# Causal attention on one core: maxima per 512-key chunk with a correction on GpSimd, and orders written by a planner

## The chip, the cores and the metric

The kernel runs on one NeuronCore of a Trainium2 chip. The metric is the device time of one execution in microseconds (us), the median of three runs. Engines are named as in the profile: PE (TensorE), PEld (its weight loads), DVE (VectorE), ACT (ScalarE), POOL (GpSimd), SP (SyncE, which issues DMAs).

## The reference

The model is four residual layers on x of 2048 tokens by 128: softmax attention, a mixture-of-experts layer, linear attention, the experts again. Only the first is touched by the change:

```python
K = jnp.einsum('bpd,ihd->biph', x, W_K)      # 16 heads of 64; Q, V alike
scores = jnp.einsum('biph,biqh->biqp', K, Q)
scores = jnp.where(mask[None, None, :, :], scores, NEG_INF)   # causal
attn = jax.nn.softmax(scores / np.sqrt(d_head).astype(np.float32), axis=-1)
z = jnp.einsum('biph,biqp->biqh', V, attn)
out = jnp.einsum('bqf,df->bqd', z_flat, W_O)
x = x + out                                   # its input was layernorm(x)
```

## The kernel before

`attention` works on 8 pairs of heads, one after the other. Within a pair, `STEPS` = 8 steps `j` each take two rows of 128 queries (2j and 2j+1) for both heads: four units `u`. A row's keys 0 to its own are cut into chunks of 512 (`BANK`), so a unit has n = 1, 1, 2, 2, 3, 3, 4, 4 chunks in steps 0 to 7; a pair has 80 chunks with 34,816 columns.

A chunk's path is: *score* on PE (L438 and L441, the high and the low part of q by k, and L440, which adds the causal mask to the last chunk) into one of `RING` = 5 PSUM banks; its maximum on DVE (L265 into `cmax`); once a unit's chunks are all there, L268 makes `nmax`, the row's negated maximum; the exponentials on ACT (L358, into `prob`, with the sum of each chunk in `esum`). `prob` has two sets of four tiles, by the step's parity.

When a step's exponentials are done, its key *groups* of 256 keys follow, j+1 of them: *turn* (L451, four transposes for each head into PSUM bank 5 or 6), the copies of these into `probT` (ACT at L365 for head 0, DVE at L274 for head 1; two buffers for each head), and *value* (L468, four products with v that write 64 rows each, in PSUM bank 7). After the last group ACT copies z (L369, *leave*), PE multiplies with `wo_bd` (L476, *out*: two products of 256 columns, one half for each head, into bank 7 as well), and DVE scales each head's half by the reciprocal sum `rinv` and adds it to x (L293, four instructions).

The order on each engine is one list for all pairs (`issue_order`), by a fixed rule: step j-1's turns and values are spread evenly between the scores of step j and what follows. The next pair's projections (*project* L485, *vproject* L494) come after all scores of a pair. POOL makes constants at the start and then does nothing in this layer.

## Time and profile before

| | us |
|---|---|
| runs | 1418.26 median of 3 (1417.16 to 1418.97) |
| the profiled execution's own time | 1418.09 |
| span, from its first instruction to its last | 1416.4 |
| attention stage, main part | 34 to 1080 |
| PE busy over the span | 1241.6 (88%) |
| DVE, ACT, POOL busy | 959.1, 793.5, 144.2 |

The profile is of one execution. Its span is the time between the first and the last instruction; its own time is 1.7 us longer. Busy time of PE is the union of matmuls whose ends are modelled, so it says when PE had work and not how close it was to its peak. Idle time before an instruction is put down to the engine that released it.

### The profile page before, as it was taken

The page shows a single profiled execution, that of the slowest core. Times are in us where ns is not written, and L with a number is a line of the kernel's source. Part 1 is how long each engine was busy: PE and PEld are TensorE (multiplying, and loading weights), DVE is VectorE, ACT ScalarE, POOL GpSimd, SP SyncE. Part 2 cuts the span into 40 slices and gives each one's busy share as a digit, 9 for nine tenths or more (in the row PEclk, how much of TensorE's full clock was granted, in tenths as well). Part 3 has the DMA queues.
Part 4 walks back from the last instruction along what each step waited for, and adds up shares of the span by engine and source line. Part 5 has one row for each costly group of instructions (what it writes and reads, how often), then busy time and mean ns, then how long its engine had stood idle before and what let it go on. Part 6 is the DMA issues. An engine that isn't in the chain of part 4 may idle for free. (4 is left out here: it accounts for less than half of the span.)

```text
span 1416.4 us, 22644 instructions
## 1 busy us (share of the span) xinstructions
PE 1241.6 (88%) x7936; PEld 856.4 (60%) x7936; DVE 959.1 (68%) x2284; ACT 793.5 (56%) x2146; POOL 144.2 (10%) x174
## 2 busy tenths in 40 slices
PE   5999999999999999999999999999996294886285
PEld 3666666666667666666666576666664292443285
DVE  5776777677767767776777677667764263998254
ACT  5766566666657666666666666666652162232043
POOL 1000000000000000000000000000000553553433
PEclk9999999999999999999999999999996596997588
DMA  3950200020001002000200020020000121000023
GB/s 102 140 133 1 60 1 1 1 60 1 1 22 39 1 1 60 1 1 1 60 1 1 16 46 1 0 60 1 1 1 1 49 64 47 0 0 0 27 59 95
DMA packets 52677, 41.07 MB, mean 29 GB/s; under 512 B 14177, under 2 KB 41442, under 8 KB 52578
## 3 DMA queue, kind: packets, MB, share of 16 engines
q1 hardware_dynamic: 50018, 34.50, 11.6%
q0 software_dynamic: 2560, 5.26, 1.1%
q8 instruction: 60, 0.98, 0.3%
q14 instruction: 39, 0.32, 0.1%
HBM read 13.49 MB, written 9.48 MB: 16 GB/s over the span
## 5 line engine op out<-in xcount | busy, mean ns | idle before, releaser
L265 DVE TENSOR_REDUCE at_cmax<-at_ps 128x1 f32<-128x512 f32 (+3 forms) x576 | 350.0, 619 | 169.0 <-PE at_ps L441 167.5
L358 ACT ACTIVATE at_prob<-at_ps,at_nmax 128x512 f32<-128x512 f32 (+3 forms) x640 | 391.8, 622 | 56.4 <-DVE at_nmax L268 53.6
L451 PE MATMUL at_ps<-ident,at_prob 128*128 128x128 f32 x2176 | 307.2, 275 | 19.0 <-DVE at_probT L274 9.6
L451 PEld LDWEIGHTS at_ps<-ident,at_prob 128*128 128x128 f32 x2176 | 249.1, 140 | 91.5 <-issue 25.5
L468 PE MATMUL at_ps<-at_probT,at_v 128*64 128x256 f32 (+1 forms) x2304 | 295.0, 379 | 3.9 <-DVE at_probT L274 3.3
L365 ACT ACTIVATE at_probT<-at_ps 128x512 f32<-128x512 f32 (+1 forms) x288 | 165.3, 574 | 228.0 <-PE at_ps L451 226.5
L438 PE MATMUL at_ps<-at_k_st,at_q_parts 128*128 128x512 f32 (+3 forms) x640 | 283.4, 443 | 8.2 <-ACT at_prob L358 7.2
L441 PE MATMUL at_ps<-at_k_st,at_q_parts 128*128 128x512 f32 (+3 forms) x640 | 251.1, 394 | 0.0
L274 DVE COPY at_probT<-at_ps 128x512 f32<-128x512 f32 (+1 forms) x288 | 189.2, 657 | 69.3 <-PE at_ps L451 66.9
L468 PEld LDWEIGHTS at_ps<-at_probT,at_v 128*64 128x64 f32 x2304 | 141.7, 136 | 129.7 <-issue 51.4
L438 PEld LDWEIGHTS at_ps<-at_k_st,at_q_parts 128*128 128x128 f32 x640 | 120.8, 189 | 87.3 <-ACT at_prob L358 50.6
L358 ACT ACTIVATION_READ_ACCUMULATOR at_prob<-at_ps,at_nmax 128x1 f32 x640 | 130.4, 204 | 0.0
L441 PEld LDWEIGHTS at_ps<-at_k_st,at_q_parts 128*128 128x128 f32 x640 | 124.5, 195 | 1.5
L646 POOL IOTA f_xn<- 128x16 uint32 x2 | 0.4, 186 | 1078.2 <-POOLq L504 1069.5
L293 DVE SCALAR_TENSOR_TENSOR x<-at_ps,at_rinv,x 128x128 f32<-128x128 f32 x256 | 77.8, 346 | 21.1 <-PE at_ps L476 18.4
L797 ACT ACTIVATE f_hT<-f_ps,f_wfix 128x128 f32<-128x128 f32 x192 | 54.7, 370 | 35.6 <-PE f_ps L842 35.6
L476 PE MATMUL at_ps<-at_wo_bd,at_zT 128*128 128x256 f32 x256 | 67.1, 384 | 2.0 <-ACT at_zT L369 2.0
L835 PE MATMUL f_ps<-ident,f_xs 128*128 128x128 f32 x48 | 14.3, 299 | 56.7 <-DMA f_xs<-slots_in 56.7
L440 PE MATMUL at_ps<-at_maskb,at_identb 128*128 128x128 bf16 x256 | 58.9, 230 | 0.0
L757 DVE COPY f_wfix<-wall 128x1156 f32 x48 | 37.1, 773 | 27.3 <-issue 26.4
L842 PE MATMUL f_ps<-f_xsT,f_wfix 128*128 128x128 f32 x384 | 55.2, 291 | 0.1
L476 PEld LDWEIGHTS at_ps<-at_wo_bd,at_zT 128*128 128x128 f32 x256 | 46.4, 189 | 13.5 <-ACT at_zT L369 7.9
(184 smaller groups left out, 1254.0 us busy)
## 6 DMA issues: line engine op xcount, KB each, us to landing
at_q_parts<-at_q_parts SPq DMA_DIRECT2D x64, 256.0 KB, 4.3
f_xs<-slots_in SPq DMA_DIRECT2D x48, 64.5 KB, 1.9
slots_in<-zeros SPq DMA_DIRECT2D x2, 1536.0 KB, 19.0
wall<-in_L_ffn_w_dram SPq DMA_DIRECT2D x1, 2048.0 KB, 18.9
wall<-in_L_ffn_w_dram SPq DMA_DIRECT2D x4, 512.0 KB, 6.6
f_got<-slots_out SPq DMA_DIRECT2D x8, 256.0 KB, 3.6
out_dram<-x SPq DMA_DIRECT2D x4, 256.0 KB, 2.4
slots_out<-f_ys,f_back POOLq DMA_INDIRECT x48, 2.2
```

The costliest lines, as they stand in the source:

```text
L265: dve.tensor_reduce(cmax[:, u % SLOTS, c:c + 1], bank, AX.X, ALU.max).then_inc(s_cmax, 1)
L274: dve.tensor_copy(probT[1][n % 2][:, 0:w], turn_ps[1][:, 0:w]).then_inc(s_probT[1], 1)
L293: last = dve.scalar_tensor_tensor(x[:, 2 * j + i, :], o_ps[i][:, h * D:(h + 1) * D], rinv[:, j % 2, 2 * i + h:2 * i + h + 1], x[:, 2 * j + ...
L358: act.activation(prob[j % 2][u % 4][:, c * BANK:c * BANK + w], ring[k % RING][:, 0:w], ACT.Exp, bias=nmax[:, u % SLOTS:u % SLOTS + 1], acc ...
L365: act.activation(probT[0][n % 2][:, 0:w], turn_ps[0][:, 0:w], ACT.Copy).then_inc(s_probT[0], 1)
L438: pe.matmul(bank[:, 0:w], q_hi[h][:, r * P:(r + 1) * P], keys, start=True, stop=False)
L440: pe.matmul(bank[:, w - P:w], identb[:, :], maskb[:, :], start=False, stop=False)
L441: last = pe.matmul(bank[:, 0:w], q_lo[h][:, r * P:(r + 1) * P], keys, start=False, stop=True)
L451: last = pe.transpose(turn_ps[h][:, b * P:(b + 1) * P], prob[j % 2][2 * i + h][:, t * P:(t + 1) * P], ident[:, :])
L468: last = pe.matmul(z_ps[rows, to:to + w], v[:, t, rows], probT[h][n % 2][:, 2 * P * b:2 * P * b + w], start=t == 0, stop=last_tile)
L476: last = pe.matmul(o_ps[i], zT[j % 2][:, i * P:(i + 1) * P], wo_bd[:, pair, :, :].rearrange("f h d -> f (h d)"), start=True, stop=True)
L842: last = pe.matmul(ps[2 + c % 2][:, f * P:(f + 1) * P], wfix[k][:, f * P:(f + 1) * P], xsT[k][:, :], start=True, stop=True)
```

## The change

**Maxima by chunk.** DVE's maximum of a chunk goes straight to `nmax` and ACT's exponential of that chunk uses it, without waiting for the other chunks of the row. What that leaves wrong is put right before the transposes: when a step's maxima are all there, DVE takes the row's (*peak*), POOL subtracts (*gap*), ACT makes the factors exp(gap) (*factor*), POOL multiplies the chunk sums with them (*weigh*), DVE adds and inverts (*total*), POOL makes one factor for each chunk, which contains the reciprocal sum as well (*scale*), and POOL multiplies every chunk of `prob` in place (*fix*, 80 for each pair, 640 in all). A turn waits for the fix of its columns.

**The output product.** Since `prob` is normalised, `wo_bd` becomes `wo`, the two products of *out* have 128 columns each, they go to a ring bank instead of bank 7, and DVE adds them with one instruction of 256 columns for each step.

**Orders and buffers.** `attention_plan` writes each engine's order from a table of steps, durations and priorities, over all pairs at once, so that steps of two pairs can mix. `probT` has `TURNED` = 4 buffers for each head. `run_of` returns one group, so each group's value products are a run of their own. The loops over the orders replace `run(order, pair, made)` on each engine.

```diff
--- before.py
+++ after.py
+RING = 5
+TURNED = 4
...
+    def run_of(j, g):
+        return [g]
...
+                w = width(u, c) / BANK
+                step(("score", p, u, c), "pe", 0.43 * w + 0.2 * (c == n - 1), ("sp", "second", p, row(u) // TPC))
+                step(("max", p, u, c), "dve", 0.15 + 0.54 * w, ("pe", "score", p, u, c), q > 1 and ("pool", "scale") + everything[q - 2])
+                step(("exp", p, u, c), "act", 0.42 + 0.42 * w, ("dve", "max", p, u, c),
+                     q > 1 and ("pe", "turn") + everything[q - 2] + (1, (j - 2) % STEPS))
+        last = ("act", "exp", p, 4 * j + 3, n - 1)
+        if n > 1:
+            step(("peak", p, j), "dve", 0.17, ("dve", "max", p, 4 * j + 3, n - 1))
+            step(("gap", p, j), "pool", 0.3, ("dve", "peak", p, j))
+            step(("factor", p, j), "act", 0.25, ("pool", "gap", p, j))
+            step(("weigh", p, j), "pool", 0.3, ("act", "factor", p, j), last)
+        step(("total", p, j), "dve", 0.35, ("pool", "weigh", p, j) if n > 1 else last)
+        step(("scale", p, j), "pool", 0.3, ("dve", "total", p, j))
+        for c in range(n):
+            for h in range(2):
+                for i in range(2):
+                    w = width(4 * j + 2 * i + h, c) / BANK
+                    step(("fix", p, j, c, h, i), "pool", 0.2 + 1.0 * w, ("pool", "scale", p, j), last)
+    groups = [(p, j, g) for p, j in everything for g in range(j + 1)]
...
+                n = groups.index((p, j, g)) - TURNED
+                step(("evict", p, j, h, g), reader, 0.16 + 0.42 * w if h == 0 else 0.14 + 0.55 * w, ("pe", "turn", p, j, h, g),
+                     n >= 0 and ("pe", "value") + groups[n][:2] + (run_of(*groups[n][1:])[-1],))
+            if g == run_of(j, g)[-1]:
+                step(("value", p, j, g), "pe", 0.85 * len(run_of(j, g)), ("act", "vproject", p, (2 * g + 1) // TPC),
+                     ("act", "evict", p, j, 0, g), ("dve", "evict", p, j, 1, g), q and ("act", "leave") + everything[q - 1])
...
+    urgent = {"pe": ["out", "project", "vproject", "score", "turn", "value"],
+              "act": ["factor", "leave", "evict", "vproject", "high", "exp"],
+              "dve": ["peak", "total", "evict", "low", "max", "add"],
+              "pool": ["gap", "weigh", "scale", "fix"], "sp": ["second"]}
...
+            s = min(ok, key=lambda s: (urgent[e].index(s[1]), can_start[s], s[2:]))
+            del can_start[s]
+            length = steps[s][0]
+            if e == "pe":
+                length += 0.16 * ((s[1] == "value") != (last == "value"))
+                last = s[1]
+                if s[1] in reader:
...
-        o_ps = [ps[RING + 2][:, 2 * D:4 * D], ps[RING + 2][:, 0:2 * D]]
...
-        wo_bd = sb("wo_bd", [P, PAIRS, 2, D])
+        wo = sb("wo", [P, PAIRS, D])
...
-        prob = [[sb(f"prob{k}{i}", [P, T - P * (i < 2)]) for i in range(4)] for k in range(2)]
+        prob = [[sb(f"prob{k}{i}", [P, T - P * (i < 2) - 2 * P * (k == 0)]) for i in range(4)] for k in range(2)]
...
-        probT = [[sb(f"probT{h}{k}", [P, BANK]) for k in range(2)] for h in range(2)]
+        probT = [[sb(f"probT{h}{k}", [P, BANK]) for k in range(TURNED)] for h in range(2)]
...
-                pool.memset(wo_bd[:, :, :, :], 0.0).then_inc(s_const, 1)
+
+                for it in order["pool"]:
+                    kind, p, j = it[:3]
+                    n, k, q = chunks(j), j % 2, STEPS * p + j
+                    if kind == "gap":
+                        pool.wait_ge(s_low, count_of["dve", "peak", p, j])
+                        pool.tensor_tensor(gap[:, k, :, 0:n], low[:, k, :].unsqueeze(2).to_broadcast([P, 4, n]), nmax[:, k, :, 0:n],
+                                           ALU.subtract).then_inc(s_gap, 1)
+                    elif kind == "weigh":
+                        pool.wait_ge(s_factor, count_of["act", "factor", p, j])
+                        pool.wait_ge(s_exp, count_of["act", "exp", p, 4 * j + 3, n - 1])
+                        pool.tensor_tensor(part[:, k, :, 0:n], factor[:, k, :, 0:n], esum[:, k, :, 0:n], ALU.mult).then_inc(s_part, 1)
+                    elif kind == "scale":
+                        pool.wait_ge(s_rinv, q + 1)
+                        share = rinv[:, k, :].unsqueeze(2).to_broadcast([P, 4, n])
+                        if n == 1:
+                            pool.tensor_copy(scale[:, k, :, 0:n], share).then_inc(s_scale, 1)
+                        else:
+                            pool.tensor_tensor(scale[:, k, :, 0:n], factor[:, k, :, 0:n], share, ALU.mult).then_inc(s_scale, 1)
+                    elif kind == "fix":
+                        _, _, _, c, h, i = it
+                        u = 2 * i + h
+                        w = width(4 * j + u, c)
+                        pool.wait_ge(s_scale, q + 1)
+                        cols = prob[k][u][:, c * BANK:c * BANK + w]
+                        pool.tensor_scalar(cols, cols, scale[:, k, u, c:c + 1], None, ALU.mult).then_inc(s_fix, 1)
...
-                            dve.tensor_reduce(cmax[:, u % SLOTS, c:c + 1], bank, AX.X, ALU.max).then_inc(s_cmax, 1)
-                            if c == chunks(u) - 1:
-                                dve.wait_ge(s_cmax, N_CMAX * pair + k + 1 - first_chunk[FIRST_MANY])
-                                dve.tensor_reduce(nmax[:, u % SLOTS:u % SLOTS + 1], cmax[:, u % SLOTS, 0:c + 1], AX.X, ALU.max,
-                                                  negate=True).then_inc(s_nmax, 1)
...
-                            for h, done in enumerate((s_acc1, s_acc2)):
-                                if h:
-                                    dve.wait_ge(s_acc1, STEPS * pair + j + 1)
-                                for i in range(2):
-                                    last = dve.scalar_tensor_tensor(x[:, 2 * j + i, :], o_ps[i][:, h * D:(h + 1) * D],
-                                                                    rinv[:, j % 2, 2 * i + h:2 * i + h + 1], x[:, 2 * j + i, :],
-                                                                    ALU.mult, ALU.add)
-                                last.then_inc(done, 1)
...
+                        dve.tensor_reduce(nmax[:, j % 2, u % 4, c:c + 1], bank, AX.X, ALU.max, negate=True).then_inc(s_max, 1)
+                    elif kind == "peak":
+                        j = it[2]
+                        n, k = chunks(j), j % 2
+                        dve.wait_ge(s_max, count_of["dve", "max", p, 4 * j + 3, n - 1])
+                        dve.tensor_reduce(low[:, k, :], nmax[:, k, :, 0:n], AX.X, ALU.min).then_inc(s_low, 1)
+                    elif kind == "total":
+                        j = it[2]
+                        n, k = chunks(j), j % 2
+                        if n == 1:
+                            dve.wait_ge(s_exp, count_of["act", "exp", p, 4 * j + 3, 0])
+                            dve.reciprocal(rinv[:, k, :].unsqueeze(2), esum[:, k, :, 0:1]).then_inc(s_rinv, 1)
+                            continue
+                        dve.wait_ge(s_part, count_of["pool", "weigh", p, j])
+                        dve.tensor_reduce(total[:, k, :], part[:, k, :, 0:n], AX.X, ALU.add).then_inc(s_total, 1)
+                        dve.wait_ge(s_total, count_of["pool", "weigh", p, j])
+                        dve.reciprocal(rinv[:, k, :], total[:, k, :]).then_inc(s_rinv, 1)
...
+                        dve.wait_ge(s_o, q + 1)
+                        if p:
+                            dve.wait_ge(s_add, q - STEPS + 1)
+                        rows = x[:, 2 * j:2 * j + 2, :]
+                        o = ring[use_of["out", p, j] % RING][:, 0:2 * D]
+                        dve.tensor_tensor(rows, o.rearrange("p (t d) -> p t d", d=D), rows, ALU.add).then_inc(s_add, 1)
...
+                        _, _, u, c = it
+                        j, h, w = u // 4, u % 2, width(u, c)
+                        if c == 0 and STEPS * p + j >= 2:
+                            act.wait_ge(s_turn[h], group(*divmod(STEPS * p + j - 1, STEPS), 0))
+                        act.wait_ge(s_max, count_of["dve", "max", p, u, c])
+                        act.activation(prob[j % 2][u % 4][:, c * BANK:c * BANK + w], ring[use_of["score", p, u, c] % RING][:, 0:w], ACT.Exp,
+                                       bias=nmax[:, j % 2, u % 4, c:c + 1],
+                                       accum_out=esum[:, j % 2, u % 4, c:c + 1]).then_inc(s_exp, 1)
+                    elif kind == "factor":
+                        j = it[2]
+                        n, k = chunks(j), j % 2
+                        act.wait_ge(s_gap, count_of["pool", "gap", p, j])
+                        act.activation(factor[:, k, :, 0:n], gap[:, k, :, 0:n], ACT.Exp).then_inc(s_factor, 1)
+                    elif kind == "evict":
+                        _, _, j, h, g = it
+                        n, w = group(p, j, g), turned(j, g) * P
+                        act.wait_ge(s_turn[0], n + 1)
+                        if n >= TURNED:
+                            act.wait_ge(s_value, value_run[n - TURNED])
+                        act.activation(probT[0][n % TURNED][:, 0:w], turn_ps[0][:, 0:w], ACT.Copy).then_inc(s_probT[0], 1)
...
+                        pe.wait_ge(s_fix, count_of["pool", "fix", p, j, 2 * g // TPC, h, 1])
+                        if n:
+                            pe.wait_ge(s_probT[h], n)
...
+                        pe.wait_ge(s_v, count_of["act", "vproject", p, (2 * end + 1) // TPC])
+                        if run_of(j, end)[0] == 0 and STEPS * p + j >= 1:
+                            pe.wait_ge(s_zT, STEPS * p + j)
+                        for h in range(2):
+                            pe.wait_ge(s_probT[h], group(p, j, end) + 1)
...
-                            for i in range(2):
-                                last = pe.matmul(o_ps[i], zT[j % 2][:, i * P:(i + 1) * P],
-                                                 wo_bd[:, pair, :, :].rearrange("f h d -> f (h d)"),
-                                                 start=True, stop=True)
-                            last.then_inc(s_o, 1)
...
+                            last = pe.matmul(ring[use_of[it] % RING][:, i * D:(i + 1) * D], zT[q % 2][:, i * P:(i + 1) * P], wo[:, p, :],
+                                             start=True, stop=True)
```

PE's order, first around the turns of step 3 of the first pair (L451 turn, L468 value, L438 and L441 score), before:

```order
L451 MATMUL at_ps<-ident,at_prob 128x128 x8
L438 MATMUL at_ps<-at_k_st,at_q_parts 128x512
L441 MATMUL at_ps<-at_k_st,at_q_parts 128x512
L451 MATMUL at_ps<-ident,at_prob 128x128 x4
L438 MATMUL at_ps<-at_k_st,at_q_parts 128x512
L441 MATMUL at_ps<-at_k_st,at_q_parts 128x512
L451 MATMUL at_ps<-ident,at_prob 128x128 x4
L468 MATMUL at_ps<-at_probT,at_v 64x256 x4
```

and now, the same step (L517 turn, L532 value, L505, L507 and L508 score, L542 out):

```order
L517 MATMUL at_ps<-ident,at_prob 128x128 x4
L542 MATMUL at_ps<-at_wo,at_zT 128x128 x2
L517 MATMUL at_ps<-ident,at_prob 128x128 x4
L505 MATMUL at_ps<-at_k_st,at_q_parts 128x512
L508 MATMUL at_ps<-at_k_st,at_q_parts 128x512
L517 MATMUL at_ps<-ident,at_prob 128x128 x4
L532 MATMUL at_ps<-at_probT,at_v 64x256 x4
L505 MATMUL at_ps<-at_k_st,at_q_parts 128x256
```

Where eight transposes stood in one run there are now two of four with *out* between them, and *out* has 128 columns instead of 256. Over the attention layer the runs of value products are 272 before and 285 now; those with a turn directly before them are 98 and 152, those with a turn directly behind them 42 and 89.

DVE's order, before (second pair, around the sums of step 4):

```order
L265 TENSOR_REDUCE at_cmax<-at_ps 128x1 x3
L268 TENSOR_REDUCE at_nmax<-at_cmax 128x1
L265 TENSOR_REDUCE at_cmax<-at_ps 128x1
L282 TENSOR_REDUCE at_rsum<-at_esum 128x4
L284 RECIPROCAL at_rinv<-at_rsum 128x4
L293 SCALAR_TENSOR_TENSOR x<-at_ps,at_rinv,x 128x128 x4
L265 TENSOR_REDUCE at_cmax<-at_ps 128x1 x2
L268 TENSOR_REDUCE at_nmax<-at_cmax 128x1
L274 COPY at_probT<-at_ps 128x512
```

and now, around the same sums:

```order
L371 COPY at_probT<-at_ps 128x512
L348 TENSOR_REDUCE at_nmax<-at_ps 128x1
L353 TENSOR_REDUCE at_low<-at_nmax 128x4
L371 COPY at_probT<-at_ps 128x384
L348 TENSOR_REDUCE at_nmax<-at_ps 128x1 x2
L362 TENSOR_REDUCE at_total<-at_part 128x4
L364 RECIPROCAL at_rinv<-at_total 128x4
L348 TENSOR_REDUCE at_nmax<-at_ps 128x1 x3
L380 TENSOR_TENSOR x<-at_ps,x 128x256
```

The reductions L268, one for each unit, are gone; in their place stand one `low` and one `total` for each step, and four scale-and-add instructions have become one.

POOL's order now, steps 6 and 7 of the second pair (before it has nothing here):

```order
L301 TENSOR_TENSOR at_gap<-at_low,at_nmax 128x16
L306 TENSOR_TENSOR at_part<-at_factor,at_esum 128x16
L313 TENSOR_TENSOR at_scale<-at_factor,at_rinv 128x16
L320 TENSOR_SCALAR at_prob<-at_prob,at_scale 128x512 x11
L301 TENSOR_TENSOR at_gap<-at_low,at_nmax 128x16
L320 TENSOR_SCALAR at_prob<-at_prob,at_scale 128x512
L320 TENSOR_SCALAR at_prob<-at_prob,at_scale 128x128
L320 TENSOR_SCALAR at_prob<-at_prob,at_scale 128x256
L320 TENSOR_SCALAR at_prob<-at_prob,at_scale 128x128
L320 TENSOR_SCALAR at_prob<-at_prob,at_scale 128x256
L306 TENSOR_TENSOR at_part<-at_factor,at_esum 128x16
L313 TENSOR_TENSOR at_scale<-at_factor,at_rinv 128x16
L320 TENSOR_SCALAR at_prob<-at_prob,at_scale 128x512 x9
```

The small steps of the next step stand between the fixes: *weigh* of the step with n = 4 waits for that step's last exponential, and the fixes behind it in the queue wait with it.

## Rows read from the trace of the kernel before

**Rows 1.** Stages: from:to, length, busy of PE, PEld, DVE, ACT, POOL, clock, DMA share.
```profile
34.00:1080.00 1046.00, 1006.98 (x6628) 680.75 (x6628) 744.43 (x1646) 672.22 (x1782) 0.19 (x1) 1.00 0.13 25
...
1160.00:1340.00 180.00, 117.11 (x464) 68.27 (x462) 125.41 (x303) 46.73 (x154) 77.77 (x94) 0.79 0.05 15
```
**Rows 2.** The same view, one head pair of 128 us.
```profile
280.00:408.00 128.00, 124.56 (x823) 84.44 (x822) 91.44 (x200) 83.69 (x222) 0.00 (x0) 1.00 0.08 17
```
**Rows 3.** Waits, 152 to 1040 us: total us, times, longest.
```profile
ACT at_prob L358 <- DVE at_nmax L268: 47.1, 58, 1.5
...
PE at_ps L451 <- DVE at_probT L274: 7.9, 10, 1.5
```
**Rows 4.** PE timeline, first and last of 2,020 rows: start us, length, instruction.
```profile
152.13 1.02 PE L485 MATMUL at_ps<-at_xnT,at_wT_q 128*128 128x512 f32 x2
...
1047.41 0.48 PE L441 MATMUL at_ps<-at_k_st,at_q_parts 128*128 128x512 f32 x1
```
**Rows 5.** The same view, 611 to 622 us.
```profile
612.34 0.39 PE L441 MATMUL at_ps<-at_k_st,at_q_parts 128*128 128x512 f32 x1
612.57 0.49 PE L451 MATMUL at_ps<-ident,at_prob 128*128 128x128 f32 x3
612.81 0.31 PE L438 MATMUL at_ps<-at_k_st,at_q_parts 128*128 128x128 f32 x1
...
613.15 0.51 PE L451 MATMUL at_ps<-ident,at_prob 128*128 128x128 f32 x3
613.59 1.08 PE L468 MATMUL at_ps<-at_probT,at_v 128*64 128x256 f32 x8
614.61 0.50 PE L438 MATMUL at_ps<-at_k_st,at_q_parts 128*128 128x512 f32 x1
614.94 0.40 PE L441 MATMUL at_ps<-at_k_st,at_q_parts 128*128 128x512 f32 x1
615.27 0.87 PE L468 MATMUL at_ps<-at_probT,at_v 128*64 128x256 f32 x8
616.07 0.50 PE L438 MATMUL at_ps<-at_k_st,at_q_parts 128*128 128x512 f32 x1
...
618.24 1.08 PE L476 MATMUL at_ps<-at_wo_bd,at_zT 128*128 128x256 f32 x4
619.15 0.60 PE L451 MATMUL at_ps<-ident,at_prob 128*128 128x128 f32 x4
```
**Rows 6.** Timeline of all engines, end of the attention stage.
```profile
1052.23 0.70 ACT L358 ACTIVATE at_prob<-at_ps,at_nmax 128x512 f32<-128x512 f32 x1
...
1063.97 1.08 PE L468 MATMUL at_ps<-at_probT,at_v 128*64 128x256 f32 x8
...
1064.99 1.09 PE L451 MATMUL at_ps<-ident,at_prob 128*128 128x128 f32 x8
...
1066.02 1.08 PE L468 MATMUL at_ps<-at_probT,at_v 128*64 128x256 f32 x8
...
1073.34 1.25 DVE L293 SCALAR_TENSOR_TENSOR x<-at_ps,at_rinv,x 128x128 f32<-128x128 f32 x4 [2.80 <-PE at_ps L476]
```
**Rows 7.** The same view, the opening.
```profile
21.55 5.27 PE L485 MATMUL at_ps<-at_xnT,at_wT_k 128*128 128x512 f32 x8 [2.44 <-ACT at_xnT L346]
...
36.75 0.30 PE L438 MATMUL at_ps<-at_k_st,at_q_parts 128*128 128x128 f32 x1 [0.37 <-issue]
```
**Rows 8.** Groups by line and shape, 34 to 1080 us: busy us, mean ns, idle before.
```profile
L293 DVE SCALAR_TENSOR_TENSOR x<-at_ps,at_rinv,x 128x128 f32<-128x128 f32 x256 | 77.8, 346 | 21.1 <-PE at_ps L476 18.4
...
L268 DVE TENSOR_REDUCE at_nmax<-at_cmax 128x1 f32<-128x4 f32 x64 | 10.1, 157 | 2.2
```
**Rows 9.** The same columns, GpSimd's groups of the whole span.
```profile
L968 POOL TENSOR_TENSOR li_outer<-li_qk,li_v 128x1152 f32<-128x1152 f32 x16 | 35.5, 2222 | 44.1 <-DVE li_qk L994 44.1
...
L962 POOL TENSOR_TENSOR li_state<-li_state,li_fresh 128x144 f32<-128x144 f32 x16 | 7.9, 491 | 1.7 <-POOL li_fresh L958 1.0
...
L43 POOL TENSOR_SCALAR_AFFINE_SELECT ident<-ident 128x128 f32<-128x128 f32 x1 | 0.3, 294 | 0.1
```

More of the change, by code:

```diff
@@ L71, in attention @@
-    N_V = NC
-    V_FIRST = N_SC + N_PJ
-    V_BANKS = [RING - 2, RING - 1] * (N_V // 2)
-    BANKS = [use % RING for use in range(V_FIRST)] + V_BANKS
-    def back_of(j):
-        items = []
-        for g in range(j + 1):
-            items += [("turn", j, 0, g), ("turn", j, 1, g)]
-            if g:
-                items += [("value", j, g - 1), None]
-        return items + [("value", j, j), None, ("leave", j)]
-    def spread(items, weights):
-        ends = [round(len(items) * sum(weights[:i]) / sum(weights)) for i in range(len(weights) + 1)]
-        return [items[a:b] for a, b in zip(ends, ends[1:])]
@@ L140, in attention @@
-    order, last_order = ([it for it in issue_order(projections) if it] for projections in (True, False))
-    opening = [(step, i) for i in range(N_PJ) for step in ("project", "low")] + [("vproject", m) for m in range(N_V)]
+    order, row, chunks, width, turned, run_of = attention_plan(PAIRS, NT, NC, TPC)
+    uses = [it for it in order["pe"] if it[0] in ("score", "project", "vproject", "out")]
+    use_of = {it: n for n, it in enumerate(uses)}
+    count_of = {}
+    for e in order:
+        ran = {}
+        for it in order[e]:
+            ran[it[0]] = ran.get(it[0], 0) + 1
+            count_of[(e,) + it] = ran[it[0]]
@@ L143, in attention, with group @@
+    def group(p, j, g):
+        return p * STEPS * (STEPS + 1) // 2 + j * (j + 1) // 2 + g
+    value_run = {}
+    for it in order["pe"]:
+        if it[0] == "value":
+            for g in run_of(it[2], it[3]):
+                value_run[group(it[1], it[2], g)] = count_of[("pe",) + it]
     with ExitStack() as ctx:
@@ L321, in _ @@
-                run(opening, 0, 0)
-                for pair in range(PAIRS - 1):
-                    run(order, pair, pair + 1)
-                run(last_order, PAIRS - 1, PAIRS)
+                    elif kind == "low":
+                        _, _, c, i = it
+                        cols = slice(c * BANK, (c + 1) * BANK)
+                        bank = ring[use_of["project", p, c, i] % RING]
+                        dve.wait_ge(s_hi, count_of["act", "high", p, c, i])
+                        for h in range(2):
+                            here, there = slice(DH * h, DH * (h + 1)), slice(DH * (1 - h), DH * (2 - h))
+                            if i == 0:
+                                last = dve.tensor_tensor(k_st[h][there, cols], bank[here, :], k_st[h][here, cols].bitcast(F32), ALU.subtract)
+                                continue
+                            last = dve.scalar_tensor_tensor(q_lo[h][here, cols], bank[here, :], SCALE, q_hi[h][here, cols].bitcast(F32),
+                                                            ALU.mult, ALU.subtract)
+                        last.then_inc(s_lo, 1)
@@ L497, in _ @@
[L497 to L500 removed]
+                        last.then_inc(s_value, 1)
+                    elif kind == "out":
+                        j = it[2]
+                        q = STEPS * p + j
+                        free_bank(it)
+                        pe.wait_ge(s_zT, q + 1)
+                        for i in range(2):
+                            last = pe.matmul(ring[use_of[it] % RING][:, i * D:(i + 1) * D], zT[q % 2][:, i * P:(i + 1) * P], wo[:, p, :],
+                                             start=True, stop=True)
+                        last.then_inc(s_o, 1)
+                    elif kind == "project":
+                        _, _, c, i = it
+                        free_bank(it)
+                        pe.matmul(ring[use_of[it] % RING][:, :], wT["kq"[i]][:, p, :], xnT[:, c * BANK:(c + 1) * BANK],
+                                  start=True, stop=True).then_inc(s_proj, 1)
+                    elif kind == "vproject":
+                        m = it[2]
+                        free_bank(it)
+                        for b in range(TPC):
+                            t = m * TPC + b
+                            last = pe.matmul(ring[use_of[it] % RING][:, b * P:(b + 1) * P], xnT[:, t * P:(t + 1) * P], wT["v"][:, p, :],
+                                             start=True, stop=True)
+                        last.then_inc(s_vproj, 1)
```

449 lines of the change are left out of this document (188 added, 261 removed).

## The prediction

> **What bounds the kernel now.** I read the busy time by stage first, then one head pair of it, the waits, and last the timeline of PE. The attention stage's main part takes 1046 us, 74% of the span, with PE busy for 1006.98, DVE for 744.43 and ACT for 672.22; the granted clock is 1.00, the upper of its two levels, so 2.4 GHz [rows 1]. Pairs repeat each 128 us: PE 124.56, DVE 91.44, ACT 83.69 of them [rows 2]. So this stage is bound by PE's queue, and DVE and ACT (71% and 65%) cost only where PE waits for them. A busy PE can also be one that starts its next matmul late. To see how much that is, I took all 2,020 merged rows of PE's timeline between 152 and 1048 us [rows 4], took the time from each start to the next, and sorted it by the pattern (what stood before, what runs, what follows). Taking a pattern's time at its fastest fifth as its price without waiting, the prices add up to 837 us and the excess over them to 58 us: 6.4%, 8.2 us of each pair, 66 us of the stage. The waits name the causes: ACT's exponentials for a row's maximum (47.1 us in all), which holds PSUM banks that PE wants, and PE's transposes for the copies out of the turn banks [rows 3]. The remaining 120 us of a pair are matmuls in order.
>
> **The change, part by part.**
>
> *The output product.* The two products of 256 columns take 0.91 us from start to start [rows 5]. Value products, also f32, do four of 256 columns in 0.80 us when two run side by side in the two halves of the array [rows 5], so one alone streams for about 0.40 to 0.43. Two of 128 columns then cost half of 0.86: 64 steps x 0.43 = **27 us off** PE, which is on the path for the whole stage. The bounds are 20 (the last step and the pair ends partly hide it) and 30.
>
> *Waits.* The exponential of a chunk no longer waits for its row; the copies have four buffers instead of two; *out* leaves bank 7, so that the next step's values need not wait for DVE's additions; DVE loses 192 small reductions of 157 ns (30 us) and changes 256 instructions of 346 ns (77.8 us busy) [rows 8] into 64 of twice the columns, at most 0.69 us each or 44 us. DVE goes from 92 us of a pair to about 84. Against that stand new waits of turns for POOL. The gain has the bounds 66 us (all waits gone) and minus 30 (below nothing: each of 64 steps may wait 0.5 us for the chain); I take **30 off**, a little under half of what is there, since the fix of a step can only start when its last exponential is done, which is a new late spot at each step.
>
> *Neighbours on PE.* Three transposes before a score cost 0.24 us (612.57 to 612.81) and before a value run 0.44; a value run then takes 1.02 with transposes before it and 0.80 in one place with a score before it, where the score pays 0.33 instead of 0.23 [rows 5]. Over the timeline a value run between scores took 0.80 in a third of the cases and 1.01 in the others, so moving a turn between score and values costs 0.22 in one third and nearly nothing in the rest: 0.1 us. The orders have 240 such neighbourhoods of turns and values instead of 140, and 13 more value runs at 0.35: 10 + 4.5, of which I take **10 on**; bounds 2 and 22. Turns among scores cost the same in any mix: by the patterns' prices eight transposes in a run and two scores behind them take 1.79 us, two runs of four with a score behind each 1.80 [rows 4].
> The Trainium skill, TensorEngine Tiling (Array Packing), Key Properties, says that changing the tiling mode drains TensorE, while another tile of the same mode does not. By that rule only value runs count (64 rows each), not who their neighbour is, and the term would be 13 x 0.35, about 4.5 us instead of 10; the rows agree on the drain at a value run but show the neighbour's price besides.
>
> *GpSimd's work.* No row shows a multiplication by a column of factors on POOL. The nearest are its tensor-tensor operations: 491 ns for 144 columns and 2222 for 1152 [rows 9], so 1.72 ns a column and 0.24 us fixed; 512 columns make 1.12 us. From below there is the select over 128 columns with one input in 0.29 us [rows 9], against 0.46 by the line: two thirds of it, 0.72 us. I take 1.1, the line, since it is a multiplication. A pair is 80 x 0.24 + 34,816 x 0.00172 = 79 us, plus 20 small steps at up to 0.46 = 9: 88 us of a pair, against some 118 of PE (120 without waits, 3.4 less for *out*, 1.3 more for neighbours). It is covered by PE's work, and while it is covered costs **nothing**. Without cover: step 7 alone is 16 x 0.24 + 7936 x 0.00172 = 17.5 us of fixes, and PE's turns and values of that step are 8 x 2.05 = 16.4 (1063.97 to 1066.02 is one group [rows 6]); the cover is the next pair's projections and scores.
> The Trainium skill, GPSIMD Engine Reference, Performance versus the Vector engine, has 769 ns measured for 512 elements of a tight loop with one input. An estimate by that figure makes POOL's pair 68 x 0.35, some 24 us, shorter, and the end below 16 x 0.35 or 5.6 us: the sum would come to 1364. No row here shows it.
>
> *The opening.* The first score starts at 36.75 us, 15.2 us after the first projection [rows 7], since all projections precede it. Now it waits only for the first chunk's. The same matmuls remain, so the gain is idle time alone: **4 off**, bounds 0 and 9.
>
> *The end.* In the last pair nothing follows step 7. From the last exponential's end (1052.9) to x (1074.6) it is 21.7 us [rows 6]. Now: *weigh* and *scale* at 0.49 each [rows 9] and two small steps of DVE at 0.16 [rows 8], 1.3; fixes 17.5; then the last turn 0.4, values 0.8 and *out* 0.5 [rows 5], two copies by ACT 1.0 and the addition 0.7 [rows 6, 8], 3.4: 22.2, and step 6's fixes may still be queued before: **3 on**, bounds 0 and 12.
>
> *At nothing:* *peak*, *gap*, *factor* (48 of each, beside exponentials; without that cover 0.16 + 0.49 us, and for the factor at most the 0.70 of an exponential of 512 columns [rows 6], 1.35 us a step, 65 us in all), the memset gone from POOL's start, and everything after the attention stage, where neither work nor order changes.
>
> Sum: -27 - 30 + 10 - 4 + 3 = -48 against the profiled execution's 1418.09, thus **1370 us**. The median of the runs is 1418.26, 0.2 us away, so nothing is corrected.
>
> **The rivals.**
>
> *POOL's chain eats the gain* (every step's first turn waits). In the order *weigh* of the next step stands before fixes of this one, and waits for the next step's last exponential. What speaks for it: the engines run their lists strictly in order, and the planner's durations (ACT 0.84 us for an exponential of 512 columns, a mask 0.2 us) aren't those of the trace. Against it: PE has scores to do meanwhile. Then the waits stay as they are or grow by some: 1400, between 1390 and 1416.
>
> *The plan works fully.* All old waits go, and new ones don't come, as the planner only places a turn where its fix is done: 30 us more off than forecast, 1340.
>
> *GpSimd becomes the bound: slower.* Mechanism: the fix takes longer than by the line, because POOL reads and writes SBUF while DVE is busy for 71% of the time (the rows of the line come from a stretch with DVE at 70% as well, 125.41 of 180 us [rows 1], which speaks against it), or because one input column by a factor is slower than two tensors. The place is steps 4 to 7, the large ones. With 9 us of small steps and 19.5 of fixed cost, PE's 118 us leave 2.57 ns a column: 1.56 us for 512 columns makes POOL the bound, and about 1.7 makes the kernel as slow as now. At 1.8 a pair is 134.6 us: 8 x 6.6 = 53 us on, and 16 x 0.7 = 11 more at the end: 1482. The Trainium skill, GPSIMD Engine Reference, Specifications, says that POOL's SBUF interfaces are shared with VectorE and names as contention DVE's instructions in a 2-port mode or with two SBUF inputs. By that rule DVE's work here, which reads PSUM with at most one SBUF input, would leave the fixes alone, and this rival would rest on the second cause only.
>
> *The change doesn't do what it says:* the value runs could be merged anyway or the orders alike; the orders above show that neither is so. No chance.
>
> **How the numbers follow.** Forecast 0.58, 1370; its own range, with the waits between 12 and 48 off and the other terms half way to their bounds, is 1345 to 1395. POOL's chain 0.17, the full plan 0.13, GpSimd as bound 0.12. The range that holds 8 in 10 takes in the chain and the plan and leaves GpSimd's bound out: 1335 to 1414. About 0.2% (2.8 us) is what a measurement of this kernel can tell from no change. Faster: all of the forecast and the plan, and most of the chain, 0.85; same 0.03; slower 0.12.
>
> **What would show it.** Right: the attention stage ends near 1030 instead of 1077, a pair takes about 122 us with PE's share at 97% or more, POOL busy for 75 to 90 us of it, the fix of 512 columns at 0.7 to 1.2 us, *out* at about 0.5 us, and PE's waits for `at_prob` from POOL few and short. Wrong: fixes at 1.5 us or more, turns that wait for POOL as the longest line of the waits, DVE's 512-column reductions longer than 686 ns, or ACT's exponentials later than before despite the chunk's own maximum.

## The result, and the profile after

The changed kernel takes 1441.43 us (median of 4 runs, 1440.2 to 1442.7) beside 1417.71 for the kernel before (median of 4): a ratio of 1.0167, 95% interval 1.0154 to 1.0179. It is 24 us slower; 1370 was forecast, the range ended at 1414, and the rival that came true had a chance of 0.12. The profiled execution has a span of 1441.0 us.

The page's busy times and two of its 40-slice lines:

```profile
PE 1229.0 (85%) x7936; PEld 837.6 (58%) x7936; DVE 891.8 (62%) x1948; ACT 797.3 (55%) x2192; POOL 1038.3 (72%) x973
...
PE   5899998999999999999999999999987194886375
...
POOL 0787879878996888798789968887993443554343
```

In the slices that lie wholly in the attention stage POOL is busy at 0.6 or more. A stretch of 130 us in it, by stage view (length, busy of PE, PEld, DVE, ACT, POOL, clock):

```profile
290.00:420.00 130.00, 121.66 (x807) 80.31 (x805) 81.04 (x154) 84.03 (x225) 110.87 (x100) 1.00 0.06 13
```

DVE went from 91.44 us in 128 [rows 2] to 81.04 in 130 and PE from 124.56 to 121.66: both have less to do in a pair, and the time is longer. POOL is busy for 110.87 of 130 us, 85%. Its groups by shape, in the columns of [rows 8]:

```profile
L320 POOL TENSOR_SCALAR at_prob<-at_prob,at_scale 128x512 f32<-128x512 f32 x448 | 694.3, 1569 | 4.7
L320 POOL TENSOR_SCALAR at_prob<-at_prob,at_scale 128x384 f32<-128x384 f32 x64 | 80.0, 1249 | 0.8
L320 POOL TENSOR_SCALAR at_prob<-at_prob,at_scale 128x256 f32<-128x256 f32 x64 | 59.7, 932 | 0.0
...
L320 POOL TENSOR_SCALAR at_prob<-at_prob,at_scale 128x128 f32<-128x128 f32 x64 | 39.1, 612 | 0.1
```

A fix of 512 columns takes 1569 ns where the forecast had 1.1 us. From 128 to 512 columns it is 957 ns more, 2.49 ns a column, with 0.29 us fixed. The tensor-tensor line of [rows 9] had 1.72 and 0.24. The waits of the whole span (total, times, longest), where [rows 3] stood before:

```profile
PEld at_ps L517 <- POOL at_prob L320: 122.8, 179, 1.9
...
POOL at_gap L301 <- DVE at_low L353: 55.7, 20, 5.1
...
PE at_ps L517 <- POOL at_prob L320: 50.3, 88, 1.5
...
ACT at_prob L423 <- DVE at_nmax L348: 41.7, 78, 1.4
...
POOL at_part L306 <- ACT at_prob L423: 26.9, 19, 2.6
```

The line that was named as a sign of failure is there: transposes (L517) that wait for POOL's `at_prob`, 50.3 us by PE's matmuls and 122.8 by its weight loads. The exponentials' wait for maxima is only a little lower: 41.7 us over the whole span, after 53.6 in the kernel before. POOL itself waits as well, for `low` at each step and for the last exponential. The end of the stage, in the columns of [rows 6]:

```profile
1066.81 0.67 ACT L423 ACTIVATE at_prob<-at_ps,at_nmax 128x512 f32<-128x512 f32 x1
...
1069.76 0.23 POOL L313 TENSOR_TENSOR at_scale<-at_factor,at_rinv 128x16 f32<-128x16 f32 x1
1070.09 24.06 POOL L320 TENSOR_SCALAR at_prob<-at_prob,at_scale 128x512 f32<-128x512 f32 x16
...
1082.51 1.09 PE L517 MATMUL at_ps<-ident,at_prob 128*128 128x128 f32 x8 [1.30 <-POOL at_prob L320]
...
1088.67 0.86 PEld L517 LDWEIGHTS at_ps<-ident,at_prob 128*128 128x128 f32 x8 [1.85 <-POOL at_prob L320]
1088.67 1.09 PE L517 MATMUL at_ps<-ident,at_prob 128*128 128x128 f32 x8 [1.39 <-POOL at_prob L320]
...
1099.22 0.42 DVE L380 TENSOR_TENSOR x<-at_ps,x 128x256 f32<-128x256 f32 x1 [2.37 <-PE at_ps L542]
```

After the last exponential (it ends at 1067.48) POOL does 16 fixes in 24.06 us, and PE starts transposes when it lets them: 1.30 and 1.39 us of idle time before them. From the last exponential's end to x it is 32.2 us, after 21.7 before. The first score, where [rows 7] has it at 36.75:

```profile
31.34 0.43 PE L505 MATMUL at_ps<-at_k_st,at_q_parts 128*128 128x128 f32 x1
```

Laid end to end: the first score comes 5.4 us earlier, the stretch from there to the last exponential's end is 20.0 longer (1036.1 after 1016.2), the end 10.5 longer: together 25 us, which is the whole difference of the spans (24.6). Behind the attention stage both traces have 341.4 us, so nothing there takes part.

One reading of the forecast must be mended first. A pair doesn't take 128 us. From the first projection of one pair to that of the next PE's timeline has 130.2 us in the kernel before, each time alike but for the first pair, and in the changed one 130.0 to 134.4 over the last five, a mean of 132.1. (A pair's length is taken over these last five in the experiments too.) By the same patterns and prices as in the forecast, PE's work of a pair is 121.8 us before and 118.7 now, and what goes beyond it 8.4 and 13.4. So the work fell by more than forecast (3.1 us for each pair; the forecast had 2.1) and the waits rose by 5 where they should have fallen by 3.7. How a pair splits into work and waits depends on how the patterns are drawn, by 1 to 2 us; that the waits rose does not. Of the 93 us beyond the prices in 919 us of this trace, 47 lie between a score and a turn.

### The profile page after: what moved, and what is told of

Read it like the earlier page. It is cut to its first block and busy times, and to the rows that moved or that the text cites. A ratio compares the mean times of both kernels' runs of the same rounds, so it can differ in the third digit from the quotient of the medians.

```text
span 1441.0 us, 24550 instructions
## 1 busy us (share of the span) xinstructions
PE 1229.0 (85%) x7936; PEld 837.6 (58%) x7936; DVE 891.8 (62%) x1948; ACT 797.3 (55%) x2192; POOL 1038.3 (72%) x973
## 5 line engine op out<-in xcount | busy, mean ns | idle before, releaser
L320 POOL TENSOR_SCALAR at_prob<-at_prob,at_scale 128x512 f32<-128x512 f32 (+3 forms) x640 | 867.0, 1377 | 5.6
L348 DVE TENSOR_REDUCE at_nmax<-at_ps 128x1 f32<-128x512 f32 (+3 forms) x640 | 376.8, 606 | 174.3 <-PE at_ps L508 171.1
L423 ACT ACTIVATE at_prob<-at_ps,at_nmax 128x512 f32<-128x512 f32 (+3 forms) x640 | 393.3, 624 | 42.8 <-DVE at_nmax L348 41.7
L517 PE MATMUL at_ps<-ident,at_prob 128*128 128x128 f32 x2176 | 338.5, 278 | 63.3 <-POOL at_prob L320 50.3
L517 PEld LDWEIGHTS at_ps<-ident,at_prob 128*128 128x128 f32 x2176 | 249.1, 140 | 188.5 <-POOL at_prob L320 122.8
L532 PE MATMUL at_ps<-at_probT,at_v 128*64 128x256 f32 (+1 forms) x2304 | 297.9, 380 | 3.9 <-DVE at_probT L371 3.0
L505 PE MATMUL at_ps<-at_k_st,at_q_parts 128*128 128x512 f32 (+3 forms) x640 | 283.9, 444 | 5.2 <-ACT at_prob L423 2.5
L508 PE MATMUL at_ps<-at_k_st,at_q_parts 128*128 128x512 f32 (+3 forms) x640 | 252.9, 395 | 0.0
L532 PEld LDWEIGHTS at_ps<-at_probT,at_v 128*64 128x64 f32 x2304 | 140.8, 136 | 111.1 <-issue 65.9
L505 PEld LDWEIGHTS at_ps<-at_k_st,at_q_parts 128*128 128x128 f32 x640 | 121.4, 190 | 69.8 <-issue 38.0
L508 PEld LDWEIGHTS at_ps<-at_k_st,at_q_parts 128*128 128x128 f32 x640 | 125.1, 195 | 1.6
L714 POOL DMA_INDIRECT slots_out<-f_ys,f_back x48 | 47.1, 981 | 63.6 <-DVE f_ys L823 51.0
L853 ACT ACTIVATE f_hT<-f_ps,f_wfix 128x128 f32<-128x128 f32 x192 | 54.7, 370 | 33.9 <-PE f_ps L898 33.9
L707 POOL DMA_INDIRECT slots_in<-f_xn,f_pos_u x32 | 31.4, 981 | 55.3 <-DVE f_pos_u L798 46.2
L1024 POOL TENSOR_TENSOR li_outer<-li_qk,li_v 128x1152 f32<-128x1152 f32 x16 | 35.5, 2220 | 43.1 <-DVE li_qk L1050 43.1
L507 PE MATMUL at_ps<-at_maskb,at_identb 128*128 128x128 bf16 x256 | 59.2, 231 | 0.0
```

The source lines that it names most:

```text
L320: pool.tensor_scalar(cols, cols, scale[:, k, u, c:c + 1], None, ALU.mult).then_inc(s_fix, 1)
L348: dve.tensor_reduce(nmax[:, j % 2, u % 4, c:c + 1], bank, AX.X, ALU.max, negate=True).then_inc(s_max, 1)
L423: act.activation(prob[j % 2][u % 4][:, c * BANK:c * BANK + w], ring[use_of["score", p, u, c] % RING][:, 0:w], ACT.Exp, bias=nmax[:, j % 2, ...
L505: pe.matmul(bank[:, 0:w], q_hi[h][:, r * P:(r + 1) * P], keys, start=True, stop=False)
L507: pe.matmul(bank[:, w - P:w], identb[:, :], maskb[:, :], start=False, stop=False)
L508: pe.matmul(bank[:, 0:w], q_lo[h][:, r * P:(r + 1) * P], keys, start=False, stop=True).then_inc(s_score, 1)
```

## The experiments

Each is an edit of the changed kernel, with the orders written anew by its planner where the plan is touched. The kernel before took 1417.15 to 1417.78 us beside them.

**1. Almost no work in the fixes (e1_narrow).**

```diff
-                        cols = prob[k][u][:, c * BANK:c * BANK + w]
+                        cols = prob[k][u][:, c * BANK:c * BANK + 1]
```

> Edit: each fix on GpSimd multiplies one column of its chunk instead of all (so most of the correction and of the normalisation is left out); orders, waits and small steps stay. Theory P (the time of the fixes, 1.57 us for 512 columns, holds up the transposes): PE's priced work of 118 us a pair remains and waits fall from 13 us a pair to 3 to 5, so 1350 to 1370 us. Theory C (the chain of small steps between the engines, not the fixes, makes the transposes late): the chain stays, 1415 to 1441. Theory O (the orders and their neighbours on PE cost more than before): 1425 or more.

Measured: 1374.08 us, ratio to the kernel before 0.9694 (0.9678 to 0.971). The fixes:

```profile
L320 POOL TENSOR_SCALAR at_prob<-at_prob,at_scale 128x1 f32<-128x1 f32 x640 | 164.5, 282 | 5.6
```

All waits, orders and small steps are the same; only the length of the fixes is gone, and with it 67 us. A pair takes 124.2 us. So neither the chain of small steps nor the orders make the kernel slower than before. The time stays 4 us above the expectation's upper end of 1370; no run here shows what these 4 us are. The edit also changes the values that the later layers get, but behind the attention stage this trace has 340 us, after 341 in the changed kernel.

**2. The fix in another form (e2_tt).** The output is complete here.

```diff
-                        pool.tensor_scalar(cols, cols, scale[:, k, u, c:c + 1], None, ALU.mult).then_inc(s_fix, 1)
+                        pool.tensor_tensor(cols, cols, scale[:, k, u, c:c + 1].to_broadcast([P, w]), ALU.mult).then_inc(s_fix, 1)
```

> Edit: the fix as a tensor-tensor multiplication with the factor broadcast along the row, same order. By the line through the tensor-tensor rows of the linear attention a fix of 512 columns takes 1.12 us instead of 1.57. Theory P: the waits fall to about 6 us a pair, 1375 to 1400 us. Theory C and O: 1430 to 1441. If the fix itself is no shorter in this form (1.5 us or more), the time says nothing on them and the line was a wrong guide.

Measured: 1373.83 us, ratio 0.9688 (0.9672 to 0.9704). The fixes and a stretch of 130 us:

```profile
L320 POOL TENSOR_TENSOR at_prob<-at_prob,at_scale 128x512 f32<-128x512 f32 x448 | 452.3, 1040 | 3.8
...
L320 POOL TENSOR_TENSOR at_prob<-at_prob,at_scale 128x128 f32<-128x128 f32 x64 | 25.6, 399 | 0.1
```

```profile
290.00:420.00 130.00, 127.11 (x869) 87.68 (x869) 85.19 (x163) 88.17 (x240) 77.29 (x104) 1.00 0.07 17
```

And the turns' waits for GpSimd over the whole span, 122.8 and 50.3 us in the changed kernel:

```profile
PEld at_ps L517 <- POOL at_prob L320: 21.3, 48, 1.3
...
PE at_ps L517 <- POOL at_prob L320: 2.4, 4, 0.8
```

The same multiplication with the factor as a broadcast second tensor takes 1040 ns for 512 columns, 1.67 ns a column: two thirds of the other form. The time is that of the first experiment within 0.3 us. PE's matmuls hardly wait for GpSimd any more. With fixes of 1.04 us GpSimd's work is thus covered, as the forecast had it for 1.1, and POOL is busy for 77 of 130 us. One line changed turns a loss of 24 us into a gain of 44.

**3. Only the plan knows the length (e3_replan).**

```diff
-                    step(("fix", p, j, c, h, i), "pool", 0.2 + 1.0 * w, ("pool", "scale", p, j), last)
+                    step(("fix", p, j, c, h, i), "pool", 0.3 + 1.27 * w, ("pool", "scale", p, j), last)
```

> Edit: the planner is given 0.3 + 1.27 us for a fix instead of 0.2 + 1.0, all orders are written anew; no instruction changes. If the wrong duration in the plan is what costs (PE stands before transposes that aren't ready while others could run), 1385 to 1410 us. If GpSimd's own load is the limit (88% of a pair and in series with each step's last exponential), 1425 to 1445.

Measured: 1423.49 us, ratio 1.0044 (1.003 to 1.0058): 18 us less than the changed kernel, and still slower than before. It fell 2 us below the range expected of a pure load and 13 above that of a pure planning error, so both take part: of the 67 us that slow fixes cost, 18 come from orders written for 1.2 us, and 49 stay when the orders know. A pair then takes 130.3 us.

**4. Two groups' value products in a run (e4_pairs).**

```diff
     def run_of(j, g):
-        return [g]
+        return list(range(g // 2 * 2, min(g // 2 * 2 + 2, j + 1)))
```

> Edit: two neighbouring key groups' value products in one run, orders planned for it. Per value run the drain costs about 0.3 us, and there are some 130 runs fewer: 40 us less work on PE. Theory P: PE waits for GpSimd instead, 1425 to 1441 us, waits a pair up by 3 to 5 us. Theory that PE is still the bound and its switches are what made the change slower: 1395 to 1405.

Measured: 1416.25 us, ratio 0.9989 (0.9979 to 0.9999). That is 25 us less than the changed kernel, between the two expectations, so it decides for neither alone. The runs of value products fall from 285 to 159. A pair is 129.2 us, 2.9 less, and the transposes still wait for GpSimd, from 150 to 970 us:

```profile
PEld at_ps L517 <- POOL at_prob L320: 70.6, 107, 1.4
...
PE at_ps L517 <- POOL at_prob L320: 38.8, 78, 1.1
```

**5. The same with the fast fix (e5_tt_pairs).** Both edits, of experiments 2 and 4.

> Edit: the fix as tensor-tensor multiplication (1.04 us for 512 columns in the run before) and value products of two key groups in one run, orders planned for it. With the slow fix the pairs gave 25 us (1441.4 to 1416.3). Theory P': with the fast fix PE is the bound, each drain spared counts in full, some 130 runs x 0.3 us = 40 us: 1330 to 1342 us. Rival: POOL's chain shows again as soon as PE is faster, 1350 to 1365.

Measured: 1339.98 us, ratio 0.9447 (0.9431 to 0.9463). From experiment 2 this is 33.9 us for 126 runs fewer, 0.27 us each, where slow fixes let only 25 through. Runs, their neighbours and the orders change together here, so the 0.27 us is not split among them. A pair takes 120.0 us, so POOL's chain does not show again.

**6. And the plan knows the fast fix (e6_tt_pairs_plan).**

```diff
-                    step(("fix", p, j, c, h, i), "pool", 0.2 + 1.0 * w, ("pool", "scale", p, j), last)
+                    step(("fix", p, j, c, h, i), "pool", 0.2 + 0.85 * w, ("pool", "scale", p, j), last)
```

> Edit: as the pairs with the fast fix, and the planner is given 0.2 + 0.85 us for a fix of 512 columns, what it takes, instead of 1.2. If only the load on GpSimd counts, the same as with the old duration within 3 us. If the plan's wrong durations cost something in either direction, 5 us or more faster.

Measured: 1329.94 us, the median of three executions of 1327.9 to 1330.3, ratio 0.9381 (0.9362 to 0.9399). A fourth took 5813, which nothing here explains and which the ratio leaves out; the median of all four is 1330.12. A wrong duration in the plan costs in this direction too: 10 us, 118.4 us a pair. It is the fastest version, 88 us below the kernel before and 111 below the changed one. Its page:

```profile
PE 1166.1 (88%) x7936; PEld 854.5 (64%) x7936; DVE 877.8 (66%) x1948; ACT 794.7 (60%) x2192; POOL 734.4 (55%) x973
...
PE   5999999999999999999999999999972867886195
...
POOL 0665566757555674675566476747634334552433
```

**7. A constant for the factor (e7_constant).** This leaves out the correction and the normalisation.

```diff
-                        pool.tensor_scalar(cols, cols, scale[:, k, u, c:c + 1], None, ALU.mult).then_inc(s_fix, 1)
+                        pool.tensor_scalar(cols, cols, 0.5, None, ALU.mult).then_inc(s_fix, 1)
```

> Edit: the fix multiplies by the constant 0.5 instead of a factor for each row from SBUF (the correction and the normalisation are left out), same order. If the operand from SBUF is what makes this form slow, 512 columns take 0.6 to 1.1 us and the kernel 1374 us; if it is the form itself, 1.5 to 1.6 us and 1441 us.

Measured: one execution, 1406.99 us. The fixes:

```profile
L320 POOL TENSOR_SCALAR at_prob<-at_prob 128x512 f32<-128x512 f32 x448 | 656.6, 1492 | 4.2
...
L320 POOL TENSOR_SCALAR at_prob<-at_prob 128x128 f32<-128x128 f32 x64 | 34.0, 532 | 0.1
```

2.50 ns a column again, and 0.21 us fixed instead of 0.29. So the form is what costs, and the factor from SBUF only 0.08 us on top. The time is the surprise: 0.08 us less for each fix, 6 us of POOL's work in a pair and 49 in the layer, made the kernel 34 us faster, in a single execution. The change of values is not the reason: behind the attention stage this trace has 342 us, after 341 in the changed kernel, and the stage itself ends 37 us earlier. Near this length the fixes pass most of their time on.

**8. Two buffers instead of four (e8_tt_two).**

```diff
-TURNED = 4
+TURNED = 2
```

> Edit: as the fast fix (1373.8 us), with two buffers instead of four for the transposed probabilities, planned for it. If the four buffers are what took PE's waits away, 1385 to 1400 us; if the maxima by chunk and the planned orders did, 1372 to 1380.

Measured: 1375.03 us, ratio 0.9697 (0.9681 to 0.9713), against 1373.83 for the fast fix. The two intervals overlap, so two buffers cost nothing that can be told apart here, and far less than the 11 us or more that the first case of the expectation had.

**9. Row maxima again (e9_tt_row).** On top of the fast fix:

```diff
-                step(("exp", p, u, c), "act", 0.42 + 0.42 * w, ("dve", "max", p, u, c),
+                step(("exp", p, u, c), "act", 0.42 + 0.42 * w, ("dve", "max", p, u, n - 1),
...
-                        act.wait_ge(s_max, count_of["dve", "max", p, u, c])
+                        act.wait_ge(s_max, count_of["dve", "max", p, u, chunks(j) - 1])
```

> Edit: as the fast fix (1373.8 us), but each exponential waits for the maxima of all chunks of its row, as in the kernel before, in the plan and in the code. If the maxima by chunk are what freed PE of its old waits, 1385 to 1400 us; if the planned orders did it and would have done it with row maxima too, 1372 to 1380.

Measured: 1424.96 us, ratio 1.005 (1.0035 to 1.0066): 51 us more than with maxima by chunk, more than either theory had. Its waits:

```profile
ACT at_prob L423 <- DVE at_nmax L348: 126.4, 119, 2.3
...
POOL at_part L306 <- ACT at_prob L423: 106.8, 45, 8.0
```

And PE's:

```profile
PE at_ps L505 <- ACT at_prob L423: 24.3, 47, 1.5
```

The exponentials wait three times as long for maxima (40.0 us in the fast fix's trace, 126.4 here), and POOL waits 106.8 us for the last exponential of a step, after 45.4. On PE it is the scores that pay: they wait 24.3 us for exponentials to free a ring bank, after 2.6 in the fast fix's trace. The transposes' weight loads wait for GpSimd as long as there (21.1 and 21.3 us), so the trace shows no delay through the fixes. So in this design the maxima by chunk are worth 51 us, orders included.

**10. The plan's other durations (e10_prices).** On top of experiment 6:

```diff
-                step(("score", p, u, c), "pe", 0.43 * w + 0.2 * (c == n - 1), ("sp", "second", p, row(u) // TPC))
+                step(("score", p, u, c), "pe", 0.45 * w + 0.08 * (c == n - 1), ("sp", "second", p, row(u) // TPC))
...
-                step(("exp", p, u, c), "act", 0.42 + 0.42 * w, ("dve", "max", p, u, c),
+                step(("exp", p, u, c), "act", 0.24 + 0.42 * w, ("dve", "max", p, u, c),
```

> Edit: as the pairs with the fast fix and its right duration in the plan (1330.1 us), and the planner's durations of an exponential (0.66 us for 512 columns, as they follow each other in the trace, instead of 0.84) and of a score are set to the measured ones. If PE's remaining waits come from the plan's wrong durations, 3 to 8 us faster; if not, within 2 us.

Measured: 1334.33 us (1331.3 to 1335.4), ratio 0.9418 (0.9403 to 0.9434): 4 us slower than with the old durations (1329.94), which neither case had. The measured lengths of single instructions do not make a better plan; why was not tried.

## Why the prediction was wrong

**The step that failed is the price of a fix.** "I take 1.1, the line, since it is a multiplication" went by tensor-tensor rows, and took the line as the upper end. But the code issues a tensor-scalar instruction, of which no row showed POOL's price. It takes 1.57 us, and the fixes, put at nothing while covered, cost 67 us. The experiments settle that this is the cause: without the fixes' work, or with fixes at 1.04 us, all else equal, the kernel takes 1374, which is 4 us from the forecast. That it is so near is partly luck, since terms below miss in both directions.

**The break-even was set too high.** The third rival named the right mechanism and asked for 1.56 us to make POOL the bound and 1.7 to bring the kernel back to 1418. The runs show 1441 at 1.57 and 1407 at 1.49; a straight line between them crosses 1418 at 1.52 (an estimate, from a single execution at 1.49 and with orders written for 1.2 us; with orders that know the duration, 1.57 us gives 1423). The threshold set POOL's work against PE's time of a pair, as if POOL could work without a pause. It can't: the fixes of a step are released together by *scale*, behind the step's last exponential, so POOL waits in every step. Its own waits from 160 to 940 us of the changed kernel's trace:

```profile
POOL at_gap L301 <- DVE at_low L353: 42.1, 16, 4.6
POOL at_scale L311 <- DVE at_rinv L359: 29.1, 6, 6.0
POOL at_scale L313 <- DVE at_rinv L364: 25.7, 24, 2.1
POOL at_part L306 <- ACT at_prob L423: 20.1, 15, 2.6
```

That is 117 us of 780, 15%. Over five whole pairs POOL is busy for 85% in the changed kernel (112 us of 132.1), 86% and 87% in experiments 3 and 4, and 82% in experiment 7, where a pair still takes 127.9 us after 124.2 with the fast fix at 60%. So a load of 82 to 87% costs time here, in an engine whose work comes in bursts behind others' results. By the forecast's terms fixes of 1.56 us would have filled PE's 118 us. The work is less than that, since small steps priced at up to 0.46 us take 0.19 to 0.23, and it was too much all the same.

**What the plan says mattered.** The forecast counted the planner's durations as a reason for waits ("the planner's durations aren't those of the trace") but gave them no price. With slow fixes they cost 18 us (experiment 3), with fast ones 10 (experiment 6).

**The other terms** can be read where the fixes are covered, in experiment 2, against 1417.7:

| term | forecast | found |
|---|---|---|
| *out* at half the columns | -27 | -21: by PE's timeline 6.1 us a pair before, 3.5 now |
| waits | -30 | -21: 8.4 us of a pair before, 5.8 now |
| neighbours on PE | +10 | -6: the rest of PE's work by prices |
| the opening | -4 | -5.4 |
| the end | +3 | +6.2: 27.9 us, 21.7 before |
| sum | -48 | -47 (measured -44) |

The first three are eight times a pair's 6.0 us, 130.2 after 124.2 being the pairs in the middle. Laid end to end, this trace has 43 us between the first score and the last exponential instead of 48, which makes -42 with the opening and the end; the profiled execution is 41.5 us shorter. How the 27 us of waits and neighbours divide depends on how the patterns are drawn: with another grouping they are -14 and -13. In neither do the neighbours cost anything.

*Out* was overrated because one instance, 0.91 us from start to start, stood for all: it is 0.76 on average before and 0.44 now. The neighbours, forecast at 10 on, cost nothing in sum: with its waits included a pair's time in turns and values, from start to start, is 66.5 us before and 65.8 now. By the Trainium skill, TensorEngine Tiling (Array Packing), Key Properties, only changes of the tiling mode drain the array, which in the forecast would have made the term 4.5. That is nearer, but not what was found either; experiments 4 and 5, with 25 and 34 us for 126 such runs fewer, agree that the runs cost time.

The end was priced by the wrong path. The forecast let the step's fixes stand in line with what follows them. In experiment 2 the last fix is done at 1021.19 and x only at 1032.21: after the last exponential (1004.33) PE has 7.7 us of the step before to finish, and then 20 us of step 7's own turns and values, with idle times of 1.1 us at most among them. In the changed kernel it is the fixes: 2.6 us to the first one, 24.1 for the sixteen, 5.5 behind them, 10.5 more than before in all. There the fixes of step 6 do delay *weigh*, which the forecast mentioned and did not price, by 1.2 us.

**The chances.** A duration that no row showed decided the sign, and its range was drawn from two rows of other forms, both below what it became. Spread evenly from 0.72 to twice the line, 2.24, nearly half of it lies beyond the 1.52 us at which the kernel is as fast as before.

What stays open: how much of the 51 us of experiment 9 comes from the ring of banks and how much from the orders written anew, and why truer durations for exponentials and scores give a worse plan.

## What to carry to other kernels

Price an instruction by its own form. Where no row shows that form, the rows of its neighbours are no bounds, and if the work is a large share of an engine's time, the sign of the whole change hangs on it; try the other forms of the same operation before giving up the design. An engine that works in bursts behind others' results can hold up the rest well below 100%: here at 82 to 87%. And an order written by a planner is only as good as the duration of the step it waits for: it cost 10 to 18 us to plan for fixes of 1.2 us when they took 1.57 or 1.04.

## What the runs showed of the hardware

On GpSimd an in-place multiplication of f32 by one factor for each partition takes 1569 ns for 128x512 as tensor-scalar, 1492 with a constant, and 1040 as tensor-tensor with the factor broadcast. The Trainium skill, GPSIMD Engine Reference, Engine selection, has it that one-input operations run roughly at line rate and two-input ones are about half as fast as on VectorE; the runs show the two-input form as the faster one, here with a broadcast second input, and the measurement decides.

At the end of the stage both forms are a little faster. There 16 fixes take 24.06 us, 1.50 each; over the whole stage the 448 of them are busy for 694.3 us, 1.55 each. In the fast form, in POOL's timeline:

```profile
1005.60 15.59 POOL L320 TENSOR_TENSOR at_prob<-at_prob,at_scale 128x512 f32<-128x512 f32 x16
```

that is 0.97 us each against 452.3 / 448 = 1.01. So it is 3 to 4%. DVE is busy for 6.4 of 24.1 us there, after 64% in the pairs, but ACT is idler too, and no run separates the two. POOL's load did not lengthen DVE's 512-column reductions: 686 ns before and after.
